# The state-space stage of a two-layer kernel: state sums in 64x64 tiles, convolution on the tensor engine, C rows by DMA, late weights read in attention

## What is computed

```python
xc, z = jnp.split(jnp.einsum('btd,ed->bte', x, in_proj_w), 2, axis=-1)        # 512 channels each
conv = conv_general_dilated(xt, conv_w, ..., feature_group_count=512) + conv_b  # 4 taps, causal
xs = _silu(conv)
x_dbl = jnp.einsum('bti,oi->bto', xs, x_proj_w)                                 # 16 step rows, 16 of B, 16 of C
dt = jax.nn.softplus(jnp.einsum('btr,ir->bti', dt_r, dt_proj_w) + dt_proj_b)
a = jnp.exp(dt[..., None] * A[None, None])                                      # 16 states a channel
u = dt[..., None] * Bv[:, :, None, :] * xs[..., None]
h = associative_scan(a, u)                                                      # h[t] = a[t] h[t-1] + u[t]
y = (jnp.einsum('btis,bts->bti', h, C) + xs * D_skip) * _silu(z)
out1 = jnp.einsum('bti,di->btd', y, out_proj_w)
h = relu(s0 * concat([x, -x]) @ sign(k0)) * 2                                   # 512 -> 1024
h = relu(s1 * h @ sign(k1)) * 2;  out2 = s2 * h @ sign(k2)                      # -> 1024 -> 256
```

## Time and profile before

| | |
|---|---|
| median of 3 runs | 3841.81 us (3839.22 to 3842.86) |
| the profiled execution | 3842.5 us, its span 3840.8 us |
| mean granted PE clock | 0.969 of full speed |
| busy over the span | PE 91%, DVE 76%, ACT 58%, POOL 38% |
| attention and all before it | 0 to 2399 us |
| projection | 2399 to 2500 us |
| state space, up to the first scan | 2500 to 2582.8 us |
| state space, 8 blocks of 64 units | 2582.8 to 3824.9 us |
| the end | 3824.9 to 3840.8 us |

### The profile page before, as it was taken

The page is one execution under the profiler, slowest core; times in us unless marked ns, Lnnn a source line. Parts: engine busy times, 40 slices in busy tenths (PEclk is TensorE's granted clock), DMA queues, the critical chain, the costliest instruction groups (busy, mean ns, idle before and its releaser), DMA issues. The chain is left out here.

```text
span 3840.8 us, 59450 instructions
## 1 busy us (share of the span) xinstructions
PE 3512.2 (91%) x19540; PEld 1564.0 (41%) x19541; DVE 2916.5 (76%) x4699; ACT 2234.8 (58%) x3500; POOL 1475.8 (38%) x1795
## 2 busy tenths in 40 slices
PE   8998999699999999999999998548998999989998
PEld 5555666433333333333333332413434344334344
DVE  5553222198888888888888883748999999899898
ACT  3331222137777777777777777236766666667663
POOL 1220000113333233332333333117777677676765
PEclk9999999869999999999999999869999999999999
DMA  4432111101111111111110000320000000000000
GB/s 145 159 126 78 45 45 45 43 20 31 32 32 32 32 32 32 32 29 32 32 30 29 29 28 14 129 60 1 12 11 12 12 6 17 6 12 12 6 12 6
DMA packets 119997, 143.66 MB, mean 37 GB/s; under 512 B 24184, under 2 KB 100224, under 8 KB 119728
## 3 DMA queue, kind: packets, MB, share of 16 engines
q1 hardware_dynamic: 102832, 106.69, 9.1%
q10 hardware_dynamic: 10752, 16.78, 1.3%
q0 software_dynamic: 6144, 16.79, 1.3%
HBM read 86.98 MB, written 52.43 MB: 36 GB/s over the span
## 5 line engine op out<-in xcount | busy, mean ns | idle before, releaser
L1181 DVE TENSOR_REDUCE pmax<-psR 128x1 f32<-128x512 f32 (+3 forms) x2240 | 1362.3, 669 | 201.2 <-PE psR L1231 115.2
L1122 ACT ACTIVATE prob<-psS 128x1024 f32<-128x1024 f32 (+3 forms) x1280 | 1099.5, 904 | 362.6 <-PE psS L1283 359.2
L1906 POOL TENSOR_TENSOR hc<-h_d,crep 128x512 f32<-128x512 f32 x512 | 666.4, 1306 | 370.2 <-DVE h_d L2162 223.9
L1231 PE MATMUL psR<-kslab,qslab 48*128 48x512 bf16 (+3 forms) x2560 | 719.1, 359 | 68.4 <-DMA kslab<-k_d 29.2
L1283 PE MATMUL psS<-qslab,kslab 51*128 51x512 bf16 (+3 forms) x2560 | 647.3, 352 | 4.9 <-ACT prob L1122 4.3
L1298 PE MATMUL psVo<-prob,vaug 128*32 128x512 f32 (+3 forms) x5120 | 627.0, 545 | 0.9 <-ACT ov L1126 0.9
L2370 PE MATMUL psYd<-hc,ident 128*128 128x512 f32 x1024 | 522.7, 599 | 0.3 <-POOL hc L1906 0.2
L1054 POOL TENSOR_SCALAR_AFFINE_SELECT prob<-prob 128x256 f32<-128x256 f32 (+1 forms) x512 | 208.6, 419 | 810.7 <-ACT prob L1122 810.4
L1231 PEld LDWEIGHTS psR<-kslab,qslab 48*128 48x128 bf16 x2560 | 192.9, 94 | 781.0 <-DVE pmax L1181 536.7
L2162 DVE TENSOR_TENSOR_SCAN h_d<-a,state,psU 128x512 f32<-128x512 f32 x384 | 489.2, 1274 | 0.3
L2152 DVE TENSOR_TENSOR psU<-dtx,psX 128x512 f32<-128x512 f32 x512 | 353.9, 691 | 56.5 <-POOL dtx L1894 12.7
(11 more groups left out here) (273 smaller groups left out, 4868.6 us busy)
## 6 DMA issues: line engine op xcount, KB each, us to landing
x_e<-rows_d SPq DMA_DIRECT2D x72, 128.0 KB, 2.0
y_d<-y SPq DMA_DIRECT2D x72, 128.0 KB, 1.7
q_d<-parts SPq DMA_DIRECT2D x48, 128.0 KB
k_d<-parts SPq DMA_DIRECT2D x48, 128.0 KB
...
x<-in_L_attn_x_dram SPq DMA_DIRECT2D x8, 512.0 KB, 6.1
wg<-n_L_ffn_gate_proj_w_dram ACTq DMA_DIRECT2D x8, 512.0 KB
```

Source lines behind the costliest of these rows:

```text
L1122: act.activation(prob[g % BUFS][:, :, off:BLK], psS[g % 2][:, :, off:BLK], ACT.Exp).then_inc(prob_ready, 1)
L1181: dve.tensor_reduce(pmax[:, a].rearrange("p i c -> p (i c)")[:, lo:lo + (count - 1) * NEXT + 1:NEXT], psR[at % BANKS][:, 0:count * w].rear ...
L1231: ins = pe.matmul(dst[:, m * w:(m + 1) * w], qslab[u][rows, i * P:(i + 1) * P], kslab[u][rows, ch * BLK:ch * BLK + w], start=(m == 0), sto ...
L1906: pool.tensor_tensor(hc[:, g % CR], h[:, g % HR], crep[:, g // PAIR % SPR], ALU.mult).then_inc(hc_ready, 1)
```

## The change

- Attention: `later_loads` gives 45 DMAs for the projection's and the state-space phase's weights; SP issues two per head behind the rest, from head 2 on, into buffers that live through projection.
- Projection: `wp` and `gamma` are there already. PE turns 13 weights, ACT copies them and makes skip and tap diagonals (`skip`, `taps`) and one eighth of `w1` per block; DVE makes `w2`, `w0` and small factors. SP reads the first x and x1 of the state-space phase.
- State space: states are added pair by pair by `add_states`: two units by two row halves give four 64x64 products; the order of channels behind z and out_proj is changed to fit. The skip is a product with a diagonal. The convolution is four products with diagonals per channel tile (`cv`). C rows go from `xbc` to DRAM and are broadcast by SP's DMAs (`spread_c`). ACT writes the ReLU twice, to f16 and f32; POOL subtracts (`low_part`). ACT and POOL cut B and C, ACT carries the halo, POOL makes the rests of x, DVE multiplies by SiLU(z) out of PSUM (`gate`). `pieces` has new units. Each engine of the two phases waits for `started`, the last semaphore that SP raises.

```diff
+def later_loads(io, keep):
...
+    got = [
+        (keep["raw_in"][:, 0:CT], io["in_proj"][0:DI].rearrange("(e p) d -> p e d", p=P)),
...
+        (keep["k0"][:], io["k0"].rearrange("(k p) f -> p k f", p=P)),
+        (keep["k1"][:], io["k1"].rearrange("(k p) f -> p k f", p=P)),
+        (keep["k2"][:], io["k2"].rearrange("(k p) f -> p k f", p=P)),
+        (keep["wp"][:], io["w_proj"].rearrange("(k p) n -> p k n", p=P)),
...
+        for p in range(CT // 2):
+            rows = slice(DI + p * 2 * P + i * P, DI + p * 2 * P + (i + 1) * P)
+            got.append((keep["raw_in"][half * i:half * i + half, CT + 2 * p:CT + 2 * p + 2],
+                        io["in_proj"][rows].rearrange("(j q) d -> q j d", q=half)))
+    for c in range(CT):
+        for i in range(2):
...
+            def load_weights(n):
+                for dst, src in later[2 * n:2 * n + 2]:
+                    sp.dma_start(dst, src).then_inc(keep["later_in"], 16)
...
+        def turned():
+            got = []
+            for k in range(KD):
+                for half in range(2):
+                    got.append(([keep["raw_in"][:, half * 4 + e, k * P:(k + 1) * P] for e in range(4)],
+                                keep["winT"][:, k, half * BLK:(half + 1) * BLK], P))
+            for c in range(CT):
+                got.append(([keep["raw_out"][:, k, c * P:(c + 1) * P] for k in range(KD)], keep["woutT"][:, c, :], P))
+            for c in range(CT):
+                got.append(([keep["raw_x"][:, c * P:(c + 1) * P]], keep["wxT"][:, c, :], XD))
+            got.append(([keep["raw_dt"][:, c, :] for c in range(CT)], keep["wdtT"][:], P))
+            return got
...
+            def middle_weight(f):
+                act.wait_ge(fac_ready, 1 + CREDIT)
+                act.activation(keep["w1"][:, f], keep["k1"][:, f], ACT.Identity, scale=fac[:, 2:3], bias=fac[:, 3:4])
...
             for n in range(NBLK):
+                middle_weight(n)
+                for x in range(2 * n, 2 * n + 2):
+                    c, tap = x // NTAP, x % NTAP
+                    act.activation(keep["taps"][:, c, tap], ident[:], ACT.Copy, scale=keep["conv_w"][:, c, tap:tap + 1])
                 token_root(n)
...
+        OPS = {"xz": KD, "cv": NTAP, "xd": CT, "dt": 1, "l1": 2 * KD, "l2": 2 * FT, "l3": 4 * FT, "out": 2 * CT}
+        INPUTS = [("xz", 0), ("xz", 1), ("xz", 2), ("cv", 0), ("xz", 3), ("cv", 1), ("xz", CT), ("cv", 2), ("xz", CT + 1),
+                  ("cv", 3), ("xz", CT + 2), ("xz", CT + 3), ("xd", 0)] + [("dt", c) for c in range(PAIR)]
...
-            for f, at in enumerate((0, 2, 4, 6)):
+            for f, at in enumerate((0, 2, 4, 6, 10, 13, 15, 17)):
                 put("l1", f, at, [4])
...
-            put("l1", 4, 9, [4])
-            put("l1", 5, 12, [4])
-            if blk:
-                put("out", 1, 12, [2, 2, 2, 2])
-            put("l1", 6, 14, [4])
-            put("l1", 7, 17, [4])
+                put("out", 1, 13, [2, 2, 2, 2])
             put("l2", 0, 18, [4, 4, 4, 4])
             for f in range(1, FT):
...
+                for e, at in enumerate((5, 7, 12, 16, 49, 51, 53, 55)):
                     put("xz", e, at, [2])
-                put("xz", CT, 25, [2])
-                put("xd", 0, 30, [2, 2])
+                for c in range(CT):
+                    put("cv", c, 20 + 4 * c, [2, 2])
+                put("xd", 0, 36, [2, 2])
                 for c in range(PAIR):
-                    put("dt", c, 35 + 4 * c, [1])
-                for e in range(CT + 1, ET):
-                    put("xz", e, 48 + e - CT, [2])
+                    put("dt", c, 41 + 4 * c, [1])
             return plan
...
+            def store_c(nb):
+                sp.wait_ge(xchain, 4 * nb + 1 + CREDIT)
+                sp.dma_start(c_rows[nb % 2], xbc[NS:2 * NS]).then_inc(c_out, 16)
+            def spread_c(k):
+                if k >= SPR:
+                    sp.wait_ge(hc_ready, PAIR * (k - SPR + 1) + CREDIT)
+                if k % (2 * NS) == 0:
+                    sp.wait_ge(c_out, 16 * (k // (2 * NS)) + 16 + CREDIT)
+                sp.dma_start(crep[:, k % SPR], c_rows[k // (2 * NS) % 2, k % NS].partition_broadcast(P))\
+                  .then_inc(c_in[k % SPR], 16)
...
-                if blk:
+            store_c(0)
+            for k in range(SPREADS):
+                blk, step = k // (2 * NS), k % (2 * NS)
+                spread_c(k)
+                if step == 5 and blk:
                     for j in range(2):
                         freed(blk - 1, "l3", j)
                     load_x1(blk)
+                if step == 13 and blk:
                     send(blk - 1)
-                if blk + 2 < NBLK:
+                if step == 23 and blk + 1 < NBLK:
+                    store_c(blk + 1)
+                if step == 31 and blk + 2 < NBLK:
                     sp.wait_ge(xl_ready, 2 * blk + 4 + CREDIT)
                     freed(blk + 1, "xz", ET - 1)
...
+            def low_part(nb, kind, f):
+                s, n = PLACE[(nb, kind, f)]
+                x = low_count(nb, kind, f)
+                pool.wait_ge(free[s], n + CREDIT)
+                pool.wait_ge(high_ready, x + 1 + CREDIT)
+                hi, lo = (f1h, f1l) if kind == "l1" else (f2h, f2l)
+                pool.tensor_tensor(lo[:, f], relu[:, x % 2], hi[:, f], ALU.subtract).then_inc(low_ready, 1)
...
+            def rest(nb, part):
+                pool.wait_ge(xchain, 4 * nb + 2 * part + 1 + CREDIT)
+                if part == 0:
+                    pool.tensor_tensor(bc_rest[:], xbc[:], bc[0:2 * NS, nb % 2], ALU.subtract).then_inc(xchain, 1)
+                else:
+                    pool.tensor_tensor(bc_rest[:], bc_rest[:], bc_mid[:], ALU.subtract).then_inc(xchain, 1)
...
+            def copy_conv(nb, c):
+                s = filled(nb, "cv", c)
+                if c < PAIR and nb:
+                    act.wait_ge(y_added, 2 * NS * (nb - 1) + 1 + CREDIT)
+                    act.wait_ge(dtx_ready, CT * (nb - 1) + PAIR + CREDIT)
+                if c >= PAIR and nb >= 2:
                     act.wait_ge(ys_ready, CT * (nb - 1) + CREDIT)
...
+                act.activation(xs[:, input_tile(nb, c)], psW[s][:], ACT.Identity, bias=vec[:, 0, c:c + 1])\
+                   .then_inc(free[s], 1)
+            def silu_conv(nb, pair):
+                for c in (PAIR * pair, PAIR * pair + PAIR - 1):
+                    s, n = PLACE[(nb, "cv", c)]
+                    act.wait_ge(free[s], n + CREDIT)
+                at = input_tile(nb, PAIR * pair)
+                act.activation(xs[:, at:at + PAIR], xs[:, at:at + PAIR], ACT.Silu).then_inc(xs_ready, 1)
...
+            def cut_bc(nb, step):
+                v, R = nb % 2, 2 * NS
+                if step == 0:
+                    s = filled(nb, "xd", 0)
+                    if nb:
+                        act.wait_ge(c_out, 16 * nb + CREDIT)
+                    if nb >= 2:
+                        act.wait_ge(b_full, NS * 2 * (nb - 1) + CREDIT)
+                    act.copy(xbc[:], psW[s][0:R, :])
+                    act.copy(bc[0:R, v], psW[s][0:R, :]).then_inc(xchain, 1)
+                    act.copy(xdt[:], psW[s][R:XD, :]).then_inc(free[s], 1)
+                elif step == 1:
+                    act.wait_ge(xchain, 4 * nb + 2 + CREDIT)
+                    act.copy(bc[R:2 * R, v], bc_rest[:])
+                    act.copy(bc_mid[:], bc_rest[:]).then_inc(xchain, 1)
+                else:
+                    act.wait_ge(xchain, 4 * nb + 4 + CREDIT)
+                    act.copy(bc[2 * R:3 * R, v], bc_rest[:]).then_inc(bc_ready, 1)
...
             def high_part(nb, kind, f):
                 s = filled(nb, kind, f)
                 dst = f1h if kind == "l1" else f2h
+                n = low_count(nb, kind, f)
                 act.activation(dst[:, f], psW[s][:], ACT.Relu).then_inc(high_ready, 1)
+                if n >= 2:
+                    act.wait_ge(low_ready, n - 1 + CREDIT)
+                act.activation(relu[:, n % 2], psW[s][:], ACT.Relu).then_inc(free[s], 1)
...
+            def gate(nb, pair):
+                dve.wait_ge(y_added, NS * (2 * nb + pair + 1) + CREDIT)
+                dve.wait_ge(sz_ready, nb + 1 + CREDIT)
+                for j in range(PAIR):
+                    c = PAIR * pair + j
+                    dve.tensor_tensor(sz[:, nb % 2, c], psY[j][:], sz[:, nb % 2, c], ALU.mult).then_inc(ys_ready, 1)
...
+                elif kind == "cv":
+                    if lo == 0:
+                        freed(nb, "xz", e)
+                    for tap in range(lo, hi):
+                        ins = pe.matmul(dst[:], taps[:, e, tap], xc[:, e, tap:tap + BLK], start=(tap == 0),
+                                        stop=(tap == NTAP - 1))
...
-                if s == 0 and g >= SEG:
-                    pe.wait_ge(yg_ready, g // SEG * PAIR - PAIR + c % PAIR + 1 + CREDIT)
-                pe.wait_ge(hc_ready, g + 1 + CREDIT)
```

(19 more changed lines are left out.)

539 lines of the change are left out of this document (218 added, 321 removed).

## The result

The changed kernel takes 3724.9 us (median of 4 runs, 3723.2 to 3728.5), the kernel before beside it 3842.3: a ratio of 0.9694 (0.9679 to 0.9709). It is faster by 117, where 154 were forecast. The profiled execution has a span of 3722.0 and a mean granted clock of 0.962 (before 0.969).

| | before | forecast | after |
|---|---|---|---|
| first scan at | 2582.8 | 2559.5 | 2557.7 |
| first to end of last scan | 1242.1 | 1113 | 1148.9 |
| from there to the end | 15.9 | 13.9 | 15.5 |
| span | 3840.8 | 3686.5 | 3722.0 |

A forecast was written before the change was run, and what follows sets the result against it. DVE's own instructions were taken as the bound: eight blocks at 1057 + 44 + 12 = 1113 us against 1242. With -129, -25.3, +2 and -2, span 3840.8 became 3686.5, forecast 3687.5, range 3628 to 3765.

The forecast's parts named there:

- DVE's pace and floor: State-space blocks: DVE needs 2.00 us a unit, 133.7 us in most blocks, at least 1057 us over eight.
- The price of a pair of units: State sums on PE: four 64x64 tiles for two units take 1.10 us instead of 1.72.
- Rivals (b) and (c): State sums: tiles pack only in twos or dearer switch, 3743 to 3807, chance 0.20; four one behind another, 4177, 0.04.
- The stall in units 20 to 38: PE work there exceeds DVE's by 8.9 us; 3 us usable lead leaves 6 or 7 a block, 44 in all.
- The coupling of 1.5 a block: State-space blocks: four full in-order engines holding each other up add 1.5 us a block, 12 in all.
- POOL and ACT: State-space blocks: POOL is busy 120 us and ACT about 102 of a 133.7 us block.
- C by DMA: State-space stage: each pair's 256 KB broadcast lands in about 2.6 us, needed every 4.2 us, so cost 0.
- Rival (d): State-space stage: the C broadcast takes over 4.2 us; at 5.0 the kernel takes 3854 us; chance 0.03.
- Before the first scan: Start of the state-space stage: first scan at 2557.5 us, 25.3 earlier, bounds 20 to 30.
- Rival (e): Attention and preamble: late loads slow attention and give back the preamble's gain, +25, 3712 us; chance 0.03.
- The tail: After the last scan: two gates on POOL (2.5 us) become two on DVE (1.4), saving 2 us.
- Rival (a): State-space blocks: DVE alone sets the pace, PE's lead covers its excess, 3631 us; chance 0.15.

The follow-up runs named there:

- e_t0: Changed kernel with DVE's sign output of the finished block in unit 0 of the next block, not unit 1: 3706.7 us.
- e_t63: Changed kernel with DVE's sign output at the end of unit 63 of its own block, except in the last block: 3708.5 us.
- e_taps2: Changed kernel with two of the four tap products of each convolution tile left out in blocks 1 to 7: 3679.1 us.
- e_fill: e_best with B spread five times instead of once in units 60, 62, 0 and 2, to keep PE busy: 3684.8 us.
- e_best: Changed kernel with PE work moved toward units 56 to 63, sign output in unit 0, second pair of step products in units 3 and 5: 3680.6 us.
- e_fill2: e_best2 with 12 more repeated spreads of B a block, in units 0, 2 and 4: 3662.6 us.
- e_best2: e_best with convolutions, x projection, step products and gate half of the input products moved once more among units: 3676.1 us.
- e_csmall: Changed kernel with each broadcast of a C row, from the fifth on, carrying only 32 of 512 columns: 3726.7 us.
- e_late: Changed kernel with its 45 late loads moved from the attention to the start of the projection: 3755.4 us.

## Why the prediction was right, and where its sum was off

The direction, the likeliest case and the range (3628 to 3765) held; the forecast was 37 low. That the miss stayed so small is in part luck: the floor was 13 too high while the stalls were 49 too low. Of the signs that it named, the first scan, the landing of the C rows and the pace of the state records came as said; a block of 139.5 us did not (it is 147), nor did waits of DVE only in units 25 to 40, since those at the block's start stand outside. Step by step:

- **DVE's pace and floor.** Right: 2.00 us a unit between scans. Gates and outputs were priced at 0.70 each; two gates cost 0.96 and an output 0.43 of the pace, so the floor was 131.8, not 133.7. This error made the forecast some 13 us too slow over the stage.
- **The price of a pair of units.** Right: 1.10 forecast; from 2902.33 to 2903.35 it is 1.02, and the two taps ahead (2900.52 to 2902.33) took 1.81 where two products take 1.72, which makes 1.11. Rivals (b) and (c) fall with that. (The sums of (b) have two slips: 13 us more less the slack of 6.6 leaves 6.4 a block, not 7, and eight blocks of 156 make 1248, not 1232. Neither touches the forecast.) The 0.25 us beyond 0.86 may be the drain that the Trainium skill ("TensorEngine Tiling (Array Packing)", Key Properties) names for a change of tiling mode; no run here separates it from another cost of the tiles.
- **The stall in units 20 to 38.** This is the step that failed, by its size: 6 us a block were forecast, as 8.9 of excess less 3 of usable lead. Measured are 10.4 in units 16 to 47. The excess was right; there is no usable lead, and the late bank adds 1.4, seen in unit 18. PE gives back there, in that wait, what lead it has, and has gained little before: by my estimate units 8 to 19 hold 23.4 us of its work (six pairs with their spread 7.9, the additions' products 6.9, four l1 tiles 3.5, two input tiles 3.4, eight l2 products 1.7) against 24.9 of DVE's. e_t0 and e_t63, which reach unit 16 some 3.4 us sooner, go through it no faster (39.44 all the same), and e_taps2 shows that the rest follows PE's work one to one when some is taken away.
- **The coupling of 1.5 a block.** It named GpSimd's and ScalarE's lateness and the decay behind ACT's new wait. Little of that was seen: DVE waits for neither in a block, and in the dense stretch PE waits 0.56 us for ACT. What cost time is a wait that I did not foresee: the change moves DVE's sign output from unit 0 to unit 1, and behind it on PE are the step product, the next spread of B and the sums. The trace of before had that wait with 0.6 us in its block. Together with the half clock it cost 4.6 a block in place of 1.5: 3.5 of them go with a shorter wait while the clock still falls (e_t0); the half clock alone was 2.1 in a kernel without that wait (e_fill against e_best, and e_fill2 against e_best2). How the 4.6 divide between the two in the changed kernel was not measured. The prediction names who waits behind the moved instructions of ACT, POOL and SP, and not behind those of DVE.
- Together the stalls were 105 us where 56 were forecast: 49 more, less the 13 of the floor, is the miss of 36.
- **POOL and ACT.** POOL is busy 112.5 a block, not 120: a low part, f32 less f16 into f16, takes 1.16 there (L1952), and the state product 1.27, and with them ahead of it the engine waits for DVE. ACT is busy 100.0 (102 forecast).

```profile
L1985 POOL TENSOR_TENSOR hc<-h_d,crep x64: 1262/1272/1307, 2887.7 to 3033.1; 128x512 f32<-128x512 f32 x64
```

```profile
L1952 POOL TENSOR_TENSOR f2l<-relu,f2h x8: 1149/1157/1162, 2894.8 to 2959.6; 128x512 f16<-128x512 f32 x8
```

- **C by DMA.** Cost 0, right, and shown by e_csmall; 3.1 us to land, between 2.6 and the 4.2 that it may take. Rival (d) falls.
- **Before the first scan.** 2559.5 forecast with the projection's 2, and 2557.7 measured (its terms, 2542.0 and 15.3, make 0.2 less than it says). PE's first product of the stage starts at 2503.24 (L2280). e_late shows where the gain comes from: with the loads uncovered it is gone (2583.0, against 2582.8 in the earlier trace rows). That these two agree so closely is chance, since the first scan varies by several microseconds from kernel to kernel. Rival (e) falls.
- **The tail.** 2 us forecast, 0.4 measured. The gates went from POOL's 2.49 to DVE's 1.29, but they wait 2.92 for the sums where the skips waited 2.02. The sums run at the half clock, after PE was idle for 2.70 and 1.27 us, and take 1.99 where they take 1.09 at the full one:

```profile
3704.08 2.45 DVE L2199 TENSOR_TENSOR_SCAN h_d<-a,state,psU 128x512 f32<-128x512 f32 x2
3706.44 0.73 DVE L2215 SCALAR_TENSOR_TENSOR r<-psW,fac,x_s 128x512 f32<-128x512 f32 x1
...
3708.03 1.99 PE L2360 MATMUL psYd<-hc,ident 64*64 64x512 f32 x8 [1.27 <-POOL hc L1985]
...
3710.08 1.29 DVE L2208 TENSOR_TENSOR sz<-psYd,sz 128x512 f32<-128x512 f32 x2 [2.92 <-PE psYd L2360]
```

- **Rival (a), DVE alone.** Its price, 3631, is now the goal rather than the forecast: e_fill2 with 3662.6 goes two thirds of the way to it from the changed kernel.

What stays open: what exactly lets the clock fall at the block's start. The fill shows that keeping PE busy there prevents it, with the gaps and the light load gone together; which of the two counts was not told apart. Unit 6 of block 3 takes 4.93 us where block 2 has 2.98; the clock stays down there to about 3005, 18 us into the block, where it is back 15 us into block 2, and why was not found.
